# Two of four diagonal B tiles of a batch's last block move from VectorE to ScalarE, in a fused Mamba, cross-attention and feed-forward layer

## The reference, cut to what matters

```
dA  = exp(delta * A)                    # decay
dBu = delta * B * u                     # input, B depends on token and state only
h_t = dA_t * h_{t-1} + dBu_t            # along 512 tokens
y   = sum over states of h * C
```

## Time and profile before

| what | value |
|---|---|
| median of 3 runs | 2558.43 us |
| lowest, highest | 2555.22, 2563.75 us |
| the profiled execution | 2563.09 us, span 2561.2 us |
| PE busy | 2349.0 us (92%) |
| DVE busy | 1873.3 us (73%) |
| POOL busy | 1670.5 us (65%) |
| ACT busy | 1480.3 us (58%) |
| granted clock, mean | 0.97 |

### The profile page before, as it was taken

How to read it: one execution, slowest core, us unless ns; L and a number is a source line. 1 busy time by engine, 2 the same in 40 slices (tenths; PEclk the granted TensorE clock), 3 DMA queues, 4 the chain that set the end, 5 groups by cost and what they waited for, 6 DMA issues and landing times. The chain is left out here.

```text
span 2561.2 us, 38124 instructions
## 1 busy us (share of the span) xinstructions
PE 2349.0 (92%) x15232; PEld 1401.8 (55%) x15232; DVE 1873.3 (73%) x2182; ACT 1480.3 (58%) x2258; POOL 1670.5 (65%) x912
## 2 busy tenths in 40 slices
PE   6799999899999999999999988777999999999997
PEld 3465566566566566566656655543445445454543
DVE  3798898998898899889889888751364565466453
ACT  3587587678678678668767757731333333443332
POOL 0698899799899889889879979860331332234130
PEclk9899999999999999999999998888999999999999
DMA  4677977877888787797787787755000000000000
GB/s 135 183 156 152 234 166 169 223 169 174 214 173 180 185 203 163 158 234 159 168 224 167 168 202 149 167 116 211 1 1 33 33 2 32 33 34 1 17 17 17
DMA packets 130384, 334.24 MB, mean 130 GB/s; under 512 B 25120, under 2 KB 73760, under 8 KB 99360
## 3 DMA queue, kind: packets, MB, share of 16 engines
q0 software_dynamic: 27648, 201.34, 39.6%
q1 hardware_dynamic: 102560, 130.46, 15.3%
HBM read 112.23 MB, written 18.20 MB: 51 GB/s over the span
## 5 line engine op out<-in xcount | busy, mean ns | idle before, releaser
L865 POOL TENSOR_TENSOR mamba_ring<-mamba_ring,mamba_c_row 128x1024 f32<-128x1024 f32 x512 | 1279.6, 2654 | 67.0 <-DVE mamba_ring L754 66.6
L754 DVE TENSOR_TENSOR_SCAN mamba_ring<-mamba_ring,ps 128x512 f32<-128x512 f32 x1024 | 1172.8, 1199 | 122.0 <-PE ps L385 119.4
L598 ACT ACTIVATE mamba_ring<-mamba_delta,mamba_a_neg 128x512 f32<-128x512 f32 x1024 | 657.6, 710 | 73.2 <-DMA mamba_ring<-mamba_ring 71.8
L385 PE MATMUL ps<-mamba_diag_b,mamba_v_t 64*128 64x128 f32 x8192 | 590.2, 287 | 86.0 <-DVE mamba_ring L754 84.6
L385 PEld LDWEIGHTS ps<-mamba_diag_b,mamba_v_t 64*128 64x128 f32 x8192 | 506.1, 191 | 278.2 <-issue 142.2
L874 POOL DMA_DIRECT2D mamba_ring<-mamba_ring x192 | 180.4, 940 | 140.0 <-DMA mamba_ring<-mamba_ring 108.8
L1521 POOL TENSOR_TENSOR xf_pr<-xf_pr,xf_top 128x1232 f32<-128x1232 f32 x32 | 75.0, 2345 | 283.7 <-DVE xf_top L1439 283.7
L298 PE MATMUL ps<-mamba_xt,mamba_wu 128*128 128x512 f32 x512 | 243.3, 621 | 17.9 <-DMA mamba_wu<-w_u 9.0
L351 PE MATMUL ps<-mamba_xt,mamba_wres 128*128 128x512 f32 x512 | 247.4, 628 | 0.0
L728 DVE SCALAR_TENSOR_TENSOR mamba_u<-ps,mamba_wcv,mamba_u 128x511 f32<-128x511 f32 (+2 forms) x192 | 142.0, 740 | 98.9 <-ACT mamba_u L561 96.3
L1514 POOL TENSOR_TENSOR xf_xn<-xf_xn,xf_bo_s 128x512 f32<-128x512 f32 x32 | 39.5, 1266 | 205.2 <-PE xf_ps L1089 205.2
(11 more groups left out here) (114 smaller groups left out, 2925.4 us busy)
## 6 DMA issues: line engine op xcount, KB each, us to landing
mamba_ring<-mamba_ring POOLq DMA_DIRECT2D x192, 1024.0 KB, 8.0
mamba_c_row<-c_rows SPq DMA_DIRECT2D x32, 1024.0 KB, 15.7
mamba_wu<-w_u SPq DMA_DIRECT2D x64, 256.0 KB, 3.9
mamba_wres<-w_res SPq DMA_DIRECT2D x64, 256.0 KB, 5.6
mamba_xt<-x_t SPq DMA_DIRECT2D x8, 1024.0 KB, 13.7
mamba_xres<-x SPq DMA_DIRECT2D x32, 256.0 KB, 8.5
x<-mamba_xres SPq DMA_DIRECT2D x32, 256.0 KB, 5.0
xf_xn<-x SPq DMA_DIRECT2D x32, 256.0 KB, 4.0
```

What stands on the lines that cost most here:

```text
L385: m = nc.tensor.matmul(ps[:, 2 * s + i, tb * P:(tb + 1) * P], v_t[g % 2][i * H:(i + 1) * H, tb * P:(tb + 1) * P], diag_b[i * H:(i + 1) * H ...
L598: a = nc.scalar.activation(ring[:, q % NR, i, :], delta[:, d % EARLY, :], ACT.Exp, scale=a_neg[:, d, 2 * k + i:2 * k + i + 1])
L754: m = nc.vector.tensor_tensor_scan(ring[:, r, i, :], ring[:, r, i, :], both[:, bass.ds(i, T, 2)], 0.0, ALU.mult, ALU.add)
L865: nc.gpsimd.tensor_tensor(ring[:, q % NR], ring[:, q % NR], c_row[:, 2 * k:2 * k + 2, :], ALU.mult).then_inc(c_done, 1)
```

## The change

ACT makes tiles 1 and 2 of the next batch, in steps 2 and 3 of the last block, behind that step's decays. For each tile it takes 8 activations, one for each of 4 groups of tokens and 2 states: a copy of the 64 columns of `eye2`, scaled by a column of `b_col`, written with a stride of two elements. DVE keeps tiles 0 and 3, and makes them one step later than before: behind the scans of steps 1 and 4. The waits of PE and of `take_bcol` follow.

```diff
+    BY_DVE, BY_ACT = (0, 3), (1, 2)
...
+        diag_act = sem("diag_act")
...
                     if b == 0:
                         pe.wait_ge(diag_ready, k + 1)
-                    elif k < LOCAL:
-                        pe.wait_ge(diag_ready, NU + LOCAL * (b - 1) + k + 1)
+                    elif k in BY_DVE:
+                        pe.wait_ge(diag_ready, NU + len(BY_DVE) * (b - 1) + BY_DVE.index(k) + 1)
+                    elif k in BY_ACT:
+                        pe.wait_ge(diag_act, len(BY_ACT) * (b - 1) + BY_ACT.index(k) + 1)
                     else:
                         pe.wait_ge(diag_loaded[k], 16 * b)
...
+            def act_diag(b, k):
+                act.wait_ge(bcol_ready, b + 1)
+                act.wait_ge(dbu_ready, (b * ND - 1) * NU + k + 1)
+                for tb in range(TT):
+                    for n in range(2):
+                        m = nc.scalar.activation(diag_b[:, tb, k, :, n], eye2[:], ACT.Copy,
+                                                 scale=b_col[:, tb, 2 * k + n:2 * k + n + 1])
+                m.then_inc(diag_act, 1)
...
+                if feeds and d == 7 and k - 1 in BY_ACT:
+                    act_diag(b + 1, k - 1)
...
                 if b >= 2:
                     dve.wait_ge(diag_stored, 32 * TT * (b - 1))
+                    dve.wait_ge(diag_act, len(BY_ACT) * (b - 1))
...
-                if feeds and d == 7 and k < LOCAL:
-                    make_diag(b + 1, k)
+                if feeds and d == 7 and k - 1 in BY_DVE:
+                    make_diag(b + 1, k - 1)
```

## The result

The changed kernel takes 2547.43 us (median of 5 runs, 2541.42 to 2550.6), the kernel before 2558.43 (5 runs beside them, 2555.22 to 2564.28). The profiled execution has a span of 2547.6 us. A repeat in another set gave 2547.68 (6 runs) and a ratio of 0.9945 (0.9924 to 0.9965).

What follows compares the result with a forecast made beforehand. PE was taken to set the first pass's pace, stalled at batch changes by DVE's tiles waiting for POOL. Caught-up changes 14 plus late ones 2 gave 16 us: 2547 profiled, 2542 median, 8-in-10 range 2526 to 2558.

Steps and rivals of the forecast that it cites:

- The wait inside the instruction: A DVE multiplication of two SBUF tiles waits while POOL has ready work, through several instructions; tile 0 took up to 6.13 us.
- Rival B: At late changes DVE waits for only one POOL instruction; product 7 near 17.5 everywhere, gain 44, time 2515; chance 0.15.
- Caught-up changes: Three batch changes where POOL is caught up: tile 0 costs 0.6, product 7 starts at 17.0; 14 us saved in all.
- the margin of 0.3 us: At caught-up changes POOL stands idle for 0.3 us when DVE asks with tile 0 behind scan 1.
- I take 1 us off each, since transfers now come denser: Deduction at each of three caught-up changes for PE's waits on transfers, bringing 17.0 saved down to 14.
- in an otherwise empty stretch: Loads of C rows and other released tiles start up to 5 us earlier, where no other transfers were expected.
- reaches the end in full: A delay at a batch change is not made up later: 206.6 us from a late tile 0, 203.5 from a caught-up one.
- Late changes: Four batch changes where POOL comes late: tile 0's wait merely moves behind scan 1; gain 0.5 each, 2 in all.
- rival B's milder form: Fewer changes are late, each one turned caught-up giving 6 us more; 2528 with two or three.
- Rival C: ACT becomes the bound if strided activations cost 0.63 each; slower, 2565 to 2569; chance 0.08.
- Rival A: Tile 0's wait stays at all changes; gain of -2 to 9, time 2549 to 2560; chance 0.18.
- D: Work moves, nothing changes: moved tiles cost only 0.66, delays of tiles 0 and 3 return one step later; 2558; chance 0.04.

Runs made afterwards that it cites:

- the shift alone: Against the kernel before, all four tiles stay on DVE, each one step later, and ACT makes none: 2544.89 us, ratio 0.994.
- ACT alone: Against the kernel before, ACT makes tiles 1 and 2, while DVE keeps tiles 0 and 3 at their old steps: 2555.31 us, ratio 0.9983.

## Why the prediction was right, point by point

**The forecast**, a gain of 16 us, has the right sign and the right account of DVE's wait; the median fell by 11.0 and the seven changes by 17.6 and 5.6 in two pairs of profiles. That the first pair comes so near 16 is luck. The three changes that were caught-up in both gave 5.5, for 14 forecast; three late in both gave 6.5, for 1.5; and the sixth, late before and caught-up after by chance, gave 5.5.

**The wait inside the instruction** stands, and is shown rather than inferred: 0.66 us with a PSUM input in the middle of POOL's work, 8.02 us with two SBUF inputs through three products. The "exclusive lock" of the State Buffer page of the Trainium skill, section "SBUF: two separate sides", agrees in who competes. Read as the prediction reads it, it does not agree in how long: the loser was not let in between two instructions of the other engine while that had more to do. Rival B, which goes by that reading, is out in its full form (2515). One reading of the prediction does not stand on its row: the scans of the earlier trace rows said to run beside POOL's work ran while POOL was idle. The statement holds all the same: the pair at 665.91 above takes 2.33 us, and POOL has a `times_c` from 665.49 to 668.22 beside it.

**Caught-up changes** went as written down to the step: scan 1 at 0.4, tile 0 at 2.7 in 0.67 us, product 4 at 5.8, tile 3 at 11.1 in 0.67, product 7 at 16.9, no fall of the clock around the change itself, the margin of 0.3 us always enough in the two profiles. Product 7 gained 17.4 in the three together, for 17.0. The mis-sized term is "I take 1 us off each, since transfers now come denser". It was about 4: the stretch behind product 7 grew from 181.1 on average in these three to 184.3 to 186.6. Two premises behind it fail with it. The transfers do not start "in an otherwise empty stretch": the DMA share is 1.03 in the 40 us from t = 10 on. And that a delay "reaches the end in full" held between the two kinds of the kernel before, not for a delay taken out. From one change to the next a caught-up one went from 203.4 to 204.2 down to 201.2 to 203.5. So each gave some 2 us, not 4.7. Part of the 4 is PE's clock, which the prediction looked at only ahead of product 7. Leaving out the seventh change, behind which the clock falls several times in all four profiles of the two kernels, the stretch takes 184.3 to 184.6 in three caught-up changes where the granted clock stays full. It takes 185.0 to 186.6 in four where the clock falls to half for 3.4 to 6.8 us, some 47 us behind t = 0, after PE's waits for merged states. Which transfers hold PE up, beyond C's rows, stays open.

**Late changes** were said to gain 0.5 and gained 2.2 in the first profile (206.8 to 204.5 from change to change). The second and fifth gained 1 us or less at product 7 and 1.2 to 1.5 behind it, since PE then no longer waits for merged states; in the first, tile 0 took only 3.67 us, and product 7 gained 5.3, of which 3.0 were lost again behind it. In the repeat one took 207.7 and one 202.7, so this size is not settled to a microsecond.

**The count** was 4 of 7 caught-up and then 5, against 3 and 4 (with the third pattern counted as late, or as the table does) before. A change that turns caught-up is worth 3 us, where rival B's milder form had 6. How much of the spread of the runs is this count is not shown: the repeat of the changed kernel has one late change less, and yet its seven changes take 1.7 us longer.

**ACT** was right: 0.25 us for each activation, 2.0 for a tile, Silu done at t = 12.4 for 12.6 predicted. Rival C is out, and no price for the stride of two shows. But ACT's part was given a gain that it does not have: the shift alone brings 0.994, ACT alone 0.9983. Beside the shift alone, product 7's 4 us per caught-up change (20.8 to 16.9) are real, and the stretch behind it takes 3.5 us more; in the first six changes PE waits 2 to 3 us there for merged states where the change is caught-up, and not at all with the shift alone. Rival A (tile 0's wait stays everywhere) is out as well; D named the right thing, that the two tiles moved were the cheap ones, but drew the wrong end from it.

## What to carry to other kernels

Where a DVE instruction with two SBUF inputs shows durations far from its least, look at what POOL does beside it. Placed behind an instruction after which POOL has run dry, it costs its work; placed in POOL's row of ready work, it costs the whole row, and everything that waits for DVE with it. Undo the parts of such a change one by one before crediting the larger part of the diff: here moving operations by one step was all that the times tell, and moving two of them to another engine next to nothing. And a stall that is removed hands the time to the next thing that is late: 32 us were taken out ahead of product 7 in either pair of profiles, and 15 and 26 came back behind it, 12 and 18 of them as PE's waits for transfers.

## What the runs showed of the hardware that was not expected

DVE's wait can outlast the issue of a transfer by POOL between two products: 8.02 us, with the 1.16 us of the merge inside. Wherever a tile had waited, in any profile, it got in where POOL stood idle before its next product; the 0.30 us that POOL waits for its own product ahead of a merge's issue were enough. Where the issue came without that idle time and the next product was ready, DVE stayed out. Activations of 64 columns with a per-partition scale and an output stride of two elements took 333 to 348 ns each, 2.02 us for eight in a row, no more than the rows of contiguous ones led to expect.
